# Attention scores with T5 bias: the bias pass of two key tiles as four 32-row matmuls, and both band additions ahead of the second maximum

## The reference

```python
def layer(x):
    x = x + layernorm(attention(layernorm(x)))
    x = x + layernorm(mixture_of_8_experts(layernorm(x)))    # gelu, top 2 gates per batch
    return x

def attention(h):
    q, k, v = heads(h @ wq), heads(h @ wk), heads(h @ wv)
    scores = einsum('bhqd,bhkd->bhqk', q, k) + rel_bias[bucket(key - query)]
    return merge(einsum('bhqk,bhkd->bhqd', softmax(scores), v)) @ wo
```

## Time and profile before

| | us |
|---|---|
| median of 3 runs | 3034.44 (3033.16 to 3037.01) |
| the profiled execution | 3035.34 |
| its span, first to last instruction | 3033.6 |
| PE busy | 2843.5 (94%) |
| POOL busy | 2276.8 (75%) |
| DVE busy | 1852.2 (61%) |
| ACT busy | 1663.9 (55%) |

### The profile page before, as it was taken

The page is one execution under the profiler, slowest core; times in us unless marked ns, Lnnn a source line. Parts: engine busy times, 40 slices in busy tenths (PEclk is TensorE's granted clock), DMA queues, the critical chain, the costliest instruction groups (busy, mean ns, idle before and its releaser), DMA issues.

```text
span 3033.6 us, 49858 instructions
## 1 busy us (share of the span) xinstructions
PE 2843.5 (94%) x18785; PEld 1052.1 (35%) x18785; DVE 1852.2 (61%) x4692; ACT 1663.9 (55%) x2174; POOL 2276.8 (75%) x1033
## 2 busy tenths in 40 slices
PE   3499999999999999999999999999999999988887
PEld 2133333333333333333333333333333333322443
DVE  5465656665566656565666556565656666685676
ACT  2255555555655555555555565556555555566576
POOL 0088888888888888888988888888888888987000
PEclk8599999999999999999999999999999999999998
DMA  7000000000000000000000000000000000100001
GB/s 159 23 1 1 1 1 18 1 1 1 19 1 1 1 3 17 2 1 2 19 2 1 1 19 1 2 1 2 19 1 1 1 8 1 57 1 29 1 1 56
DMA packets 45607, 36.53 MB, mean 12 GB/s; under 512 B 21510, under 2 KB 43782, under 8 KB 45366
## 3 DMA queue, kind: packets, MB, share of 16 engines
q1 hardware_dynamic: 45366, 33.34, 4.2%
HBM read 28.39 MB, written 11.34 MB: 13 GB/s over the span
## 4 chain that ended last, share of the span: by engine, by line
PE 48%; DVE 20%; issue 18%; POOL 9%; ACT 4%; DMA 1%; SPq 1%; POOLq 0%; DVEq 0%; ACTq 0%
PE po L617 16%; PE st L587 14%; POOL acc L527 9%; PE pre L599 5%; DVE mpart L1265 4%; PE pm L555 4%; DVE st L1282 3%; PE st L817 3%; DVE pre L1262 3%; PE pm L561 2%; DVE pre L1257 2%; PE pm L647 2%; ACT prob L896 1%; PE pm L626 1%; DMA t_scratch<-w_scratch 1%
## 5 line engine op out<-in xcount | busy, mean ns | idle before, releaser
L527 POOL TENSOR_TENSOR acc<-acc,prob 128x1024 f32<-128x1024 f32 x896 | 2117.3, 2363 | 388.1 <-ACT prob L896 308.2
L896 ACT ACTIVATE prob<-st 128x1024 f32<-128x1024 f32 x1024 | 1016.6, 1022 | 911.7 <-DVE st L1282 813.8
L617 PE MATMUL po<-prob,v 128*64 128x512 f32 x4096 | 994.9, 606 | 0.0
L587 PE MATMUL st<-qk 64*128 64x512 f16 x6144 | 835.4, 378 | 21.3 <-ACT prob L896 16.7
L1257 DVE CUSTOM_DVE_ANT_0 pre<-pre,ew 128x512 f32<-128x512 f32 x448 | 300.8, 713 | 567.0 <-issue 566.9
L1262 DVE CUSTOM_DVE_ANT_0 pre<-pre,tab 128x512 f32<-128x512 f32 x704 | 475.2, 715 | 147.2 <-issue 147.1
L587 PEld LDWEIGHTS st<-qk 64*128 64x128 f16 x6144 | 293.3, 94 | 349.9 <-ACT prob L896 60.2
L617 PEld LDWEIGHTS po<-prob,v 128*64 128x64 f32 x4096 | 249.0, 136 | 442.0 <-issue 367.5
L587 PE MATMUL st<-eq,ek 64*128 64x512 f16 x2048 | 389.8, 377 | 0.0
L599 PE MATMUL pre<-qk 64*128 64x512 f16 x1600 | 311.9, 386 | 52.9 <-ACT ew L926 19.2
L1265 DVE TENSOR_REDUCE mpart<-pre 128x2 f32<-128x1024 f32 x224 | 274.0, 1223 | 98.4 <-PE pre L599 96.8
(11 more groups left out here) (189 smaller groups left out, 2350.6 us busy)
## 6 DMA issues: line engine op xcount, KB each, us to landing
t_scratch<-w_scratch SPq DMA_DIRECT2D x2, 3072.0 KB
inv_r<-inv SPq DMA_DIRECT2D x260, 1.0 KB, 1.7
y<-x SPq DMA_DIRECT2D x2, 2048.0 KB, 11.5
qk<-x SPq DMA_DIRECT2D x8, 512.0 KB, 5.6
out<-qk SPq DMA_DIRECT2D x8, 512.0 KB, 3.5
w<-w_pairs SPq DMA_DIRECT2D x8, 384.0 KB, 3.7
t2f<-t_scratch SPq DMA_DIRECT2D x8, 384.0 KB, 4.8
t<-t_scratch SPq DMA_DIRECT2D x8, 384.0 KB, 3.2
```

Source lines behind the costliest of these rows:

```text
L527: nc.gpsimd.tensor_tensor(acc[g % 2][:, :, :], a, prob[:, n % RING, :, :], ALU.add).then_inc(sum_p, 1)
L587: last = nc.tensor.matmul(st[:, 2 * (n % 2) + h, :], w[64 * h:64 * h + 64, :], t[64 * h:64 * h + 64, :], start=(r == 0), stop=(r == len(te ...
L617: last = nc.tensor.matmul(po[64 * h:64 * h + 64, :], v[:, g // CHUNKS, j, 64 * h:64 * h + 64], prob[:, n % RING, h, :], start=(s == 0), st ...
L896: nc.scalar.activation(prob[:, n % RING, :, :], st[:, 2 * (n % 2):2 * (n % 2) + 2, :], ACT.Exp).then_inc(exp_done, 1)
```

## The change

The four banks of `st` for steps n+2 and n+3 now get their far values and maxima in one pass ahead of the scores: `score_rows` issues four matmuls with 32 rows of `ek` and `eq` each, row groups 0, 32, 64 and 96, one for each head and step, with `start=True`. The three passes of each step's scores follow with `start=False`. `score_rows` stands at the top of the turn, ahead of the first piece, and waits for both exponentials, of step n and of step n+1. `ek` and `eq` hold their contents every 32 rows instead of every 64, so `max_in` issues four DMAs in place of two, and `far_rows` four instructions of 8 partitions in place of two of 32. On DVE both bands stand ahead of the second maximum, and `BAND_STEPS` has odd steps alone.

```diff
-BAND_STEPS = [3, 5, 8, 10, 13, 15]
+BAND_STEPS = [3, 5, 7, 11, 13, 15]
-M_ROW = 32
+M_ROW = 2 * QT
-    r = np.arange(128) % 64
+    r = np.arange(128) % 32
@@ max_in, on SP
-                for h in range(2):
-                    sp.dma_start(eq[64 * h + M_ROW:64 * h + M_ROW + 1, g % 2, :].rearrange("p (t q) -> p t q", q=128),
+                for k in range(4):
+                    h = k % 2
+                    sp.dma_start(eq[32 * k + M_ROW:32 * k + M_ROW + 1, g % 2, :].rearrange("p (t q) -> p t q", q=128),
                                  mrow[QT * h:QT * h + QT, :]).then_inc(m_in, 16)
@@ scores
-                         (kl[b][:, keys], qh[b][:, queries]), (ek[:, variant(c, j), :], eq[:, g % 2, :])]
+                         (kl[b][:, keys], qh[b][:, queries])]
-                                                start=(r == 0), stop=(r == len(terms) - 1))
+                                                start=False, stop=(r == len(terms) - 1))
+            def score_rows(i, n):
+                g = step_of(n)[0]
+                for d in range(2):
+                    scores_wait(i, n + d)
+                for d in range(2):
+                    j = step_of(n + d)[2]
+                    for h in range(2):
+                        k = 2 * d + h
+                        nc.tensor.matmul(st[:, k, :], ek[32 * k:32 * k + 32, variant(g % CHUNKS, j), :],
+                                         eq[32 * k:32 * k + 32, g % 2, :], start=True, stop=False)
@@ the turn on PE
                 for n in range(0, STEPS, 2):
+                    if not last or n + 2 < STEPS:
+                        score_rows(i, n + 2)
                     next_piece(n)
                     for m in (n + 2, n + 3):
                         if not last or m < STEPS:
-                            scores_wait(i, m)
                             scores(m)
                     next_piece(n + 1)
@@ far_rows on ACT (on DVE alike)
-                for h in range(2):
-                    nc.scalar.activation(eq[64 * h:64 * h + 32, buf, :].rearrange("p (t q) -> p t q", q=128),
+                for k in range(4):
+                    part = slice(32 * k, 32 * k + 2 * QT)
+                    nc.scalar.activation(eq[part, buf, :].rearrange("p (t q) -> p t q", q=128),
@@ the turn on DVE
                         bands = band(i, n + 2, bands)
-                    next_maximum(n + 1)
                     if not last or n + 3 < STEPS:
                         bands = band(i, n + 3, bands)
+                    next_maximum(n + 1)
```

More of the change, by code:

```diff
@@ L569, in scores_wait @@
                 if s == 0:
-                    pe.wait_ge(m_in, (G + 1) * 32)
+                    pe.wait_ge(m_in, (G + 1) * 64)
                     if g < 2:
-                        pe.wait_ge(far_set, (i + n // STEPS) * 4 + 2 * g + 2)
+                        pe.wait_ge(far_set, (i + n // STEPS) * 8 + 4 * g + 4)
                     if c == 0:
@@ L695, in _ @@
             pe.wait_ge(v_a, 4)
+            score_rows(0, 0)
             for n in range(2):
-                scores_wait(0, n)
                 scores(n)
@@ L899, in far_rows @@
             def far_rows(pair, buf):
-                for h in range(2):
-                    nc.scalar.activation(eq[64 * h:64 * h + 32, buf, :].rearrange("p (t q) -> p t q", q=128),
-                                         rowc[64 * h:64 * h + 32, 0:QT].unsqueeze(2).broadcast_to((32, QT, 128)), ACT.Copy,
-                                         scale=farv[64 * h:64 * h + 32, 0, bass.ds(2 * pair + h, 1)]).then_inc(far_set, 1)
+                for k in range(4):
+                    part = slice(32 * k, 32 * k + 2 * QT)
+                    nc.scalar.activation(eq[part, buf, :].rearrange("p (t q) -> p t q", q=128),
+                                         rowc[part, 0:QT].unsqueeze(2).broadcast_to((2 * QT, QT, 128)), ACT.Copy,
+                                         scale=farv[part, 0, bass.ds(2 * pair + k % 2, 1)]).then_inc(far_set, 1)
             def next_table(i, part):
@@ L1214, in far_rows @@
             def far_rows(pair, buf):
[L1217 to L1220, removed]
+                for k in range(4):
+                    part = slice(32 * k, 32 * k + 2 * QT)
+                    nc.vector.tensor_scalar(eq[part, buf, :].rearrange("p (t q) -> p t q", q=128),
+                                            rowc[part, 0:QT].unsqueeze(2).broadcast_to((2 * QT, QT, 128)),
+                                            farv[part, 0, bass.ds(2 * pair + k % 2, 1)], None, ALU.mult).then_inc(far_set, 1)
             def pair_table(pair, k):
```

## The result

| | us |
|---|---|
| before, median (range, runs) | 3034.23 (3033.16 to 3037.01, 4) |
| after, median (range, runs) | 3058.14 (3056.41 to 3060.20, 4) |
| ratio after / before | 1.0078, 95% interval 1.0060 to 1.0095 |
| profiled execution of after | 3059.07, span 3057.3 |

The change makes the kernel 24 us slower. The forecast was 3036, no difference that can be measured, with a range of 2984 to 3062; the time lies near the upper end of the range and 22 us above the forecast. Measured again beside other kernels, the changed one took 3057.34 and the one before 3033.85.

What follows compares the result with a forecast made beforehand. PE bounds the kernel, with DVE and ACT close behind between the pieces. Slot sums gave +5 us, halved to +2 for the last heads and rounding, on the median 3034.4: about 3036, range 2984 to 3062.

Steps and rivals of the forecast that it cites:

- a dearer far pass: Rival: the four 32-row matmuls don't run as one pass; 3058 at 1.25 passes, 3146 two by two; chance 0.10.
- The step on which everything rested: Attention loop: passes leave an interval DVE or ACT nearly filled, new pass lies outside; near +0.27, single +0.15, less -0.06 us.
- The old bound: Attention loop before the change: PE, busy 94% of the span, waits adding up to some 41 us of 2630.
- all three kinds: First to second piece of a turn: near 1.90, single 1.78, less 1.57 us after the change, where PE needs 1.51.
- The far pass at 0.32: Top of each of 512 turns: pass 0.216, later starts 0.01, shape change 0.093, in all 0.32 us.
- a free change: Rival: the shape change between 32 and 64 rows costs nothing, each turn 0.09 us less, 2988; chance 0.13.
- The bands: Band ahead of the second maximum: step pair 6 gains 0.39 to 0.77 us, step pair 5 pays 0.29 to 0.66.
- one set of two stands in a turn with slack: Doubled `far_rows` instructions on ACT: one added set costs nothing, the other 0.22 us in step pair 3.
- The slot sums: Turn changes over step pairs 0 to 7: 0.00, +0.24, +0.37, -0.31; +0.30 us for four slots, 16 times: +5 us.
- PE waiting ahead of the second piece: Sign of being right: PE idle there in most turns, released by the renumbered reduction lines, some 0.27 us on average.
- PE busy time down by about 60 us: Sign of being right: PE's busy time falls by about 60 us while the span stays unchanged.
- The landing of the maxima: Four `max_in` DMAs: landing at 560.6, needed from 561.1; price 0, or 64 slots by up to 0.5 us without cover.

## Why the prediction was right, and where it was off

**The number.** The stated forecast, 3036 with some 9 us to either side, was given a chance of 0.71, and 3058 lies outside it. It lies within the range because the range took in half of a dearer far pass (3058 at 1.25 passes), and the far pass was not dearer. To that extent the hit is luck: the 22 us come from terms that the prediction had at nothing or too small, named below.

**What bounds the kernel.** Right. The step on which everything rested, that the work taken out lies in an interval which DVE or ACT nearly fill and the work put in lies outside, is shown from both sides: a second far pass costs 103 us, and a shorter maximum brings 103 us with the change but 51 us without it. The old bound still counts at the top of the turn: a pass that stands there is paid in full.

**Intervals.** Right to 0.01 us in all three kinds, in nearly all turns; the exceptions are step pair 3 of slot 0 (3.51) and of slot 7 and step pair 5 of slots 2 and 7 (2.04, 1.87 and 2.04).

**The far pass at 0.32.** The mechanism was right: the change of shape between 32 and 64 rows is not free, and the four matmuls run as one pass. The size was a little off: 0.327 from the far pass to the piece, and 0.320 to 0.322 from the second piece to the values or a job in place of 0.309 to 0.312. That is 0.017 in each turn, 9 us in all. The second half of it is not a matter of the far pass: in the kernel before too (0.309 against 0.319 to the values, 0.312 against 0.322 to a job), the 0.010 appears where the second piece has waited and not where it has not. Both rivals on the far pass fall: a free change would have shown 0.23, a dearer pass over 0.35, and the doubled pass adds 0.216, one pass and not 1.25 or 1.3.

**The bands.** Step pairs 0 to 2, 4, 6 and 7 were met within 0.02 us a turn; step pair 5 was put 0.06 too low.

**The small part that was not small.** The step that failed is "one set of two stands in a turn with slack". It priced ACT's 1.4 us more by whether ACT had time, and not by what stands behind it in ACT's queue. Three queues were chained: the copy on ACT, its reader on DVE, the maximum behind that reader, and PE waiting for that. The term was 0 for slot 0 and measured 1.72 us in each of 8 pairs, 14 us. Putting the far rows behind the copy takes all of it off that turn, which shows it. The doubling is not alone in it: the band edit that moves a band from step 8 to step 7 delays the same far rows and costs 0.69 of that turn by itself, and the prediction, which followed the bands through step pairs 1, 2, 5 and 6, put nothing for it here.

**The rounding.** The slot sums gave +5 and the text took +2 "against" effects that it did not work out. By the measured turns the same terms, without the far rows, are 12 us: about 7 more than +5, the 9 us of the far pass and the wait less what the roundings of the other terms gave back. With 14 for the far rows that is the 25.6 of the table. For the last pair of heads the prediction took less than for the others, and its trace shows more (5 to 6 us against 3).

**Signs that it named.** PE waiting ahead of the second piece, released by L1279 and L1282, some 0.27 us on average: the intervals are 0.26 longer on average than PE's own 1.52, but the rows of waits name only 166 turns of 512, since they leave out short ones. PE busy time down by about 60 us: it fell by 20, because a matmul's record is 0.38 long and covers part of the gap behind it. That sign was badly chosen. The landing of the maxima: PE idled 4.0 us for it over the whole run (2.8 before), so the four DMAs cost next to nothing, as forecast.

## What to carry to other kernels

Taking work from a busy engine pays only up to the next loop that runs beside it: time that loop from its release to its next release before counting passes, and put the remaining work on the side of the gap where it can fill it (2986 us by the kind of the gap, against 3005 with the pass always behind the first piece and 3041 with it always ahead, all three with the single far-row instruction). An instruction added on a slack engine costs what waits behind it in every queue down the chain, so put it behind the one that another engine reads. And try the reordering alone first: a one-line move of the band on DVE gave 40 us, where the change that it was meant to support added some 7 to it at its best place, and the kernel as first changed is 24 us slower than the one before.

## What the runs showed of the hardware

- Four matmuls of 32 rows into four PSUM banks start within 10 ns and occupy one pass: doubled, they take 0.54 us in place of 0.33 until the next piece, one pass of 0.216 more.
- A change of the shape in use costs about 0.10 us beyond the pass of 0.216 when it is between 32 and 64 rows of the same 128 columns (0.322 into the far pass, 0.327 out of it, of which 0.01 are the starts of four), as between 64 and 128 rows (0.312). Two changes around a saved pass cancel it (1.955 against 1.953).
- From a second piece that has waited to what follows it takes 0.010 us more than from one that has not (0.320 against 0.309 to the values, 0.322 against 0.312 to a job), with the same instructions and in the kernel before too. No run tells why.
- The ACT instruction that writes 512 columns of far rows takes 0.71 us for 128, for 32 or for 8 partitions, so four of 8 take 2.93 us. The partitions made no difference here.
